# Attention kernel on one core: a unit's weighing cut into five steps of 256 columns instead of four of 128 to 512

## The reference

```python
x = x + out_proj(attention(layernorm(x)))        # 16 heads of 16, causal, 512 tokens
x = x + moe(layernorm(x))                        # 8 experts, top 2, hidden width 1024, exact GELU

scores = einsum('bhqd,bhkd->bhqk', q, k) * scale
scores = where(causal, -inf, scores)
out    = einsum('bhqk,bhkd->bhqd', softmax(scores), v)
```

## Time and profile before

| | us |
|---|---|
| timed runs, median of 3 | 976.07 |
| timed runs, lowest and highest | 970.33 and 979.5 |
| span of the profiled execution | 991.0 |
| of it PE busy | 872.7 |
| DVE busy | 722.9 |
| ACT busy | 587.6 |
| POOL busy | 461.7 |

### The profile page before, as it was taken

How to read it: one execution, slowest core, us unless ns; L and a number is a source line. 1 busy time by engine, 2 the same in 40 slices (tenths; PEclk the granted TensorE clock), 3 DMA queues, 4 the chain that set the end, 5 groups by cost and what they waited for, 6 DMA issues and landing times.

```text
span 991.0 us, 21222 instructions
## 1 busy us (share of the span) xinstructions
PE 872.7 (88%) x6870; PEld 576.0 (58%) x6870; DVE 722.9 (73%) x1658; ACT 587.6 (59%) x1079; POOL 461.7 (47%) x561
## 2 busy tenths in 40 slices
PE   4999988787788888897878898989989999999996
PEld 3655422242433434352424686879869989989875
DVE  6578878758578797969893785885766766666664
ACT  2776566656678686858776562554544455445453
POOL 2000123334425747655667546574476464544441
PEclk9999977876887978677987997999989999999998
DMA  9988667654857676575727452242223232323231
GB/s 213 293 275 256 207 180 220 177 139 120 215 168 225 172 189 183 159 191 150 201 77 232 125 120 39 46 85 51 47 36 54 50 49 46 56 50 50 36 52 19
DMA packets 146327, 130.09 MB, mean 131 GB/s; under 512 B 59344, under 2 KB 128848, under 8 KB 146096
## 3 DMA queue, kind: packets, MB, share of 16 engines
q1 hardware_dynamic: 115648, 87.51, 31.8%
q0 software_dynamic: 15680, 18.95, 12.0%
q10 hardware_dynamic: 14896, 22.28, 7.1%
HBM read 83.63 MB, written 44.80 MB: 130 GB/s over the span
## 4 chain that ended last, share of the span: by engine, by line
PE 49%; DVE 17%; issue 10%; DMA 9%; POOL 6%; SPq 5%; ACT 3%; POOLq 1%; ACTq 0%; another core or an unknown queue 0%; DVEq 0%
PE banks L769 15%; PE banks L787 14%; PE banks L582 4%; PE banks L697 3%; PE banks L685 3%; DVE arena L1230 3%; PE banks L641 2%; PE banks L572 2%; DVE weights L1384 2%; DMA weighed_values<-arena 2%; POOL out L1702 2%; DVE arena L1232 2%; POOL slot_tokens L1649 2%; PE banks L626 2%; DMA inverse_sums<-arena 2%
## 5 line engine op out<-in xcount | busy, mean ns | idle before, releaser
L991 ACT ACTIVATE arena<-banks,arena 128x256 f32<-128x256 f32 (+1 forms) x312 | 152.2, 541 | 192.9 <-issue 126.8
L769 PE MATMUL banks<-arena,weights 128*128 128x256 f16 (+1 forms) x1872 | 207.4, 266 | 11.5 <-issue 8.6
L787 PE MATMUL banks<-weights,arena 128*128 x1704 | 197.5, 275 | 3.6 <-DVE arena L1514 2.6
L769 PEld LDWEIGHTS banks<-arena,weights 128*128 x1872 | 174.0, 98 | 39.5 <-issue 16.2
L1702 POOL DMA_INDIRECT out<-arena x71 | 115.6, 1628 | 168.4 <-DVE arena L1525 131.8
L787 PEld LDWEIGHTS banks<-weights,arena 128*128 128x128 f16 x1704 | 166.4, 99 | 26.9 <-issue 6.4
L641 PE MATMUL banks<-arena 50*128 50x128 f16 (+3 forms) x512 | 126.4, 352 | 37.9 <-DMA arena<-arena 12.2
L1512 DVE TENSOR_SCALAR arena<-arena 128x512 f16<-128x512 f32 (+1 forms) x156 | 77.1, 494 | 70.6 <-ACT arena L991 58.9
L613 PE MATMUL banks<-arena 48*128 48x384 f16 (+3 forms) x512 | 103.1, 345 | 26.4 <-DVE arena L1233 9.3
L1514 DVE SCALAR_TENSOR_TENSOR arena<-arena 128x512 f16<-128x512 f32 (+1 forms) x156 | 111.0, 711 | 5.6
L641 PEld LDWEIGHTS banks<-arena 50*128 50x128 f16 x512 | 39.1, 102 | 128.7 <-issue 43.3
(11 more groups left out here) (190 smaller groups left out, 1338.9 us busy)
## 6 DMA issues: line engine op xcount, KB each, us to landing
weights<-in_L_ffn_w ACTq DMA_DIRECT2D x16, 1024.0 KB, 7.8
arena<-in_L_ffn_w SPq DMA_DIRECT2D x32, 512.0 KB
qk_parts<-weights SPq DMA_DIRECT2D x64, 128.0 KB
arena<-qk_parts SPq DMA_DIRECT2D x128, 64.0 KB, 3.2
weighed_values<-arena SPq DMA_DIRECT2D x32, 256.0 KB
token_rows<-arena SPq DMA_DIRECT2D x12, 512.0 KB, 4.3
arena<-qk_parts SPq DMA_DIRECT2D x128, 32.0 KB, 3.3
arena<-weighed_values SPq DMA_DIRECT2D x32, 128.0 KB
```

Source lines behind the costliest of these rows:

```text
L769: m = pe.matmul(bank[:, c * TILE:c * TILE + WIDTH[j]], w1[:, k, wp, f:f + P], xp[:, k, 0:WIDTH[j]], start=(i == 0), stop=(i == len(terms) ...
L787: m = pe.matmul(bank[:, c * D:(c + 1) * D], hp[:, f, c * P:(c + 1) * P], w2[:, f // (FC // 2), wp, f % (FC // 2), :], start=(f == 0 and i ...
L991: m = act.activation(h_32[r % 2][:, c, 0:WIDTH[j]], banks[:, 1 + c2, c * TILE:c * TILE + WIDTH[j]], ACT.Gelu, bias=b1_now[j % 2][:, 2 * c2 ...
```

## The change

Each unit is weighed in five steps, one behind each combined step. Step 0 and step 1 take the two halves of block 0, step 2 the first 256 columns of block 1, step 3 the last 128 columns of block 1 and the 128 of block 3, step 4 block 2. The ticks of the steps are 6, 15, 24, 33 and 43; the last unit, behind which no combined steps come, has 6, 13, 20, 27 and 34. `copy_o` goes from tick 41 to 48, `keep_o` from 51 to 55, `move_o` from 70 to 72 (not in the last unit, and `move_o` not in the last two). A step now issues eight profiled matmuls, step 3 sixteen: 48 a unit instead of 32. Waits on a number of weighings are counted in fives. The exponentials wait for just the steps that read what they overwrite.

```diff
-        W_ORDER = (0, 3, 1, 2)
+        W_STEPS = (((0, 0, 256),), ((0, 256, 512),), ((1, 0, 256),), ((1, 256, 384), (3, 0, 128)), ((2, 0, 256),))
+        W_ALL = len(W_STEPS)
+        W_READ = {0: 2, 1: 4, 3: 4, 2: 5}
...
-            for i, kt in enumerate(W_ORDER):
-                at(after + (6, 16, 24, 34)[i], "weigh", (u, kt))
-            at(after + 41, "copy_o", u)
+            last = u == UNITS - 1
+            for i in range(W_ALL):
+                at(after + ((6, 13, 20, 27, 34) if last else (6, 15, 24, 33, 43))[i], "weigh", (u, i))
+            at(after + (41 if last else 48), "copy_o", u)
...
-            at(after + 51, "keep_o", u)
-            at(after + (84 if late else 70), "move_o", u)
+            at(after + (51 if last else 55), "keep_o", u)
+            at(after + (84 if late else 72), "move_o", u)
...
-            def weigh(u, kt):
-                w.wait_ge(sem("masked"), 3 * u + (3 if kt == 2 else 2))
-                if kt == W_ORDER[0]:
+            def weigh(u, step):
+                w.wait_ge(sem("masked"), 3 * u + (3 if step == W_ALL - 1 else 2))
+                if step == 0:
...
-                for h in range(HG):
-                    a, width = PT_AT[kt], T - kt * P
-                    m = pe.matmul(banks[32 * h:32 * h + 32, O_BANK, kt * P:T], v_and_ones(u, kt, h),
-                                  p_T[u % 2][:, h, a:a + width], start=(kt == W_ORDER[0]), stop=(kt == W_ORDER[-1]),
-                                  tile_position=(0, 32 * h))
+                for kt, first_col, end_col in W_STEPS[step]:
+                    for h in range(HG):
+                        m = pe.matmul(banks[32 * h:32 * h + 32, O_BANK, kt * P + first_col:kt * P + end_col],
+                                      v_and_ones(u, kt, h), p_T[u % 2][:, h, PT_AT[kt] + first_col:PT_AT[kt] + end_col],
+                                      start=(step == 0), stop=(step == W_ALL - 1),
+                                      tile_position=(0, 32 * h), skip_group_check=True)
...
-                        w.wait_ge(sem("weighed"), TT * (u - 1))
+                        w.wait_ge(sem("weighed"), W_ALL * (u - 2) + max(W_READ[kt] for _, kt, _ in blocks))
...
-                w.wait_ge(sem("weighed"), TT * (UNITS - 1))
+                w.wait_ge(sem("weighed"), W_ALL * (UNITS - 1))
```

More of the change, by code:

```diff
@@ L886, in exponentials @@
                 for s in range(2):
+                    j, blocks = E_USES[2 * i + s]
                     if u >= 2:
-                        w.wait_ge(sem("weighed"), TT * (u - 1))
+                        w.wait_ge(sem("weighed"), W_ALL * (u - 2) + max(W_READ[kt] for _, kt, _ in blocks))
                     else:
                         w.wait_ge(sem("tops"), 2 * 2 * LATE)
-                    j, blocks = E_USES[2 * i + s]
                     w.wait_ge(sem("scored_T"), exp_use(u, 2 * i + s) + 1)
@@ L908, in copy_o @@
             def copy_o(u):
-                w.wait_ge(sem("weighed"), TT * (u + 1))
+                w.wait_ge(sem("weighed"), W_ALL * (u + 1))
                 if u > 0:
@@ L1509, in split_hidden @@
                 else:
-                    w.wait_ge(sem("weighed"), TT * UNITS)
+                    w.wait_ge(sem("weighed"), W_ALL * UNITS)
                 pair, width = slice(2 * c2, 2 * c2 + 2), slice(0, WIDTH[j])
@@ L1785, in load_v @@
                 if u >= 2:
-                    w.wait_ge(sem("weighed"), TT * (u - 1))
+                    w.wait_ge(sem("weighed"), W_ALL * (u - 1))
                 w.wait_ge(sem(f"v_store{b % 2}"), 16 * (b // 2 + 1))
```

## The result

The changed kernel takes 976.44 us (median of 20 runs, 973.28 to 984.0), the kernel before 971.9 us (20 runs, 962.09 to 979.5). The ratio is 1.0066, with a 95% interval of 1.0045 to 1.0088: 6.4 us slower, where 5.6 us faster was forecast. The time lies in the stated range, but on the other side of no change.

The account below looks back on a forecast made before the run. No engine fills attention; PE is nearest, at mean clock 0.80, DVE about as near mid-stage. +12.4 - 11 - 9 + 0 + 0 + 2 = -5.6 us on a 991.0 us span, taken as a share, gave 970.5 us; range 956 to 987.

Parts of the forecast that it names:

- The price of a step: PE's weighing in attention: 0.60 us for 256 columns at full clock, step 3 0.69 (0.60 to 0.78); +12.4 us in all.
- Part 3: PE's 17 waits at a unit's first combined step, 21.6 us, get partly filled by the added step: -11 us (0 to -17).
- Part 5: PE's wait for copy_o ahead of the next unit's first weighing stays as it is: 0, up to +6 us.
- Part 4: Fewer hollows (stretches where PE idles) in attention, so a quarter of the low-clock time goes up: -9 us (0 to -20).
- The second rival: Without the dense 512-column weighing PE's clock stays low longer in attention: +13.4 us, 989 us; chance 0.17.
- Part 7: Hand-over from attention to the experts: late loads start some 2.5 us later, partly hidden: +2 us (0 to 3).
- The first one: Rival: PE's gain in attention is waited for elsewhere, at DVE and ACT; +3.4 us, 979.4 or about 977 us; chance 0.29.
- The third one: Rival: copy_o has too short a cover before the next unit's first weighing; +0.4 us, 976.5 us; chance 0.08.
- the chance of 0.33 for faster: Chance given to the whole kernel being over 1% faster (under 966.3 us), beside same 0.46 and slower 0.21.
- the forecast's 0.46: Chance given to the main forecast of 970.5 us, own range 957 to 979, against its three rivals.

Follow-up runs that it names:

- cut_in_place: Kernel before with only the cutting: blocks 0 and 1 split, each combined step keeping its old columns behind it, 48 matmuls a unit; 1.0034 of the kernel before.
- block2_behind_fifth: Kernel before with its four uncut steps, the one of 256 columns moved from tick 34 to 40, behind the fifth combined step; 1.0028 of the kernel before.
- copy_back: Changed kernel with the fifth step at tick 40 and copy_o, keep_o and move_o at their old ticks 41, 51 and 70; 1.0049 of the kernel before.
- four_late_copy: Kernel before with its four steps, only copy_o at tick 48, keep_o at 55 and move_o at 72; 1.0015 of the kernel before.
- five_repaired: Changed kernel with copy_o, keep_o, move_o at old ticks, fifth step at 40, unit 30 at the last unit's ticks; 1.0022 of the kernel before.
- two_dense: Kernel before with its four steps at ticks 6, 6, 24, 24, so weighings stand behind the first and third combined steps only; 1.0061 of the kernel before.

## Why the prediction was wrong, step by step

- **The price of a step** was right: 0.60 us for 256 columns, and step 3 at the lower bound, 0.60. The raw cost is 9.5 us, and its reason is five separate steps a unit for four (cut_in_place), none of them the one of 512 columns that was cheap for its size. The rule of 0.21 us for each 128 columns and 0.18 on top fits three of the four forms and not 512 columns, 0.91 where it gives 1.02; the sum did not use it. The Trainium skill's rule on drains at a change of the tiling mode (TensorEngine Tiling (Array Packing), Key Properties) gave just this bound; the trace agrees that a second group in the same mode adds none (0.60 us). How much of the 0.18 us is the drain no run separates.
- **Part 3, the filled waits**, was -11 us. The waits it names did fall by 10 and 13 us, and idle ahead of first combined steps by 16 in all. The failed reasoning is "what they wait for does not depend on it". From the end of one unit's scores run at the same time the eight issues of the next load and its landing, the tops and DVE's reductions, and PE meets them at the first and at the fifth combined step. A wait filled at the first is met again at the fifth, as block2_behind_fifth shows with 25 and 10 us turned into 10 and 28.
- **Part 5, the cover of the copy**, was 0, with +6 us as its end. The wait grew from 2.6 to 10.3 us. The step that failed is the look at ACT's queue: "the copy stands at the same place against the exponentials" is true, and the stages between them, at ticks 42 to 47, were not looked up. Yet copy_back, four_late_copy and five_repaired show no cost of that wait that can be told from nothing: in copy_back ACT's work came before an exponential that PE waits for instead. Parts 3 and 5 together came to -6.8 us of idle time, against -11.
- **Part 4, the clock**, -9 us, is the step that decides the sign, and it did not come: low clock in attention 172 us in the mean of two profiles before and 176 after, and in the timed runs 0.9025 against 0.9084 and 0.9042. Without this term the forecast's own sum is +3.4 us. Nothing was measured that ties the number of hollows to the low time. That a gap ahead of a fall can be seen does not make a gain of filling it, when as much idle time turns up elsewhere. The second rival did not come either; two_dense, the opposite of the change, has 175 us.
- **Part 7, the hand-over**, was +2 (0 to 3) and measured 3 to 5: the loads start 4 us later against the end of attention and not 2.5. Behind them in SP's queue stands the write of unit 30's values, and their read-back comes 5.6 to 6.0 us behind the last weighing in the kernels with the late hand-over, 1.4 to 3.3 in both profiles of the kernel before. Which of the two delays costs the time no run separates.

With these sizes the sum is +9.5 - 6.8 + 0 + 4 = +6.7 us, beside 6.4 measured. The 4 is the middle of what the runs on the hand-over give. That the two agree to 0.3 us is luck: two profiles of one kernel differ by 4 us in idle time, and the hand-over is known to 3 at best. The runs bear out the parts by themselves: with the hand-over repaired five steps take 1.0019 and 1.0022, so all in attention together is some 2 us, neither a gain nor clearly a loss.

None of the named rivals was right as a whole. The first one's sum without the clock, +3.4, was nearest and had the right sign on the span; that the gain is waited for elsewhere is what the runs show, but the place is not DVE or ACT at their limit. The third one's sign came (10 us of waits for the copy) without its price. And the chance of 0.33 for faster does not follow from the text: somewhat under half of the forecast's 0.46 is at most 0.23.

Not tried: whether an earlier issue of the q and k loads on another queue would shorten the loop itself.

## What to carry to other kernels

Before counting a filled wait as a gain, follow the awaited thing back to where it starts: if that is an earlier point of the waiting engine's own loop, work moved within the loop only moves the wait. When a tick or a queue position is moved, list every stage of the same engine between the old and the new place, and read the one iteration that hands over to the next stage by itself; one line there was worth 3 to 5 of the 6.4 us. And before a clock share is given a price, compare the granted clock of many timed runs, or at least two profiles of the same kernel. Last, ask of an experiment whether it contains the cost it is to test: cut_in_place had the cut's matmuls and none of its PE time.

## What the runs showed of the hardware that was not expected

The granted clock's share over a stage is not a property of the kernel alone: the same program had 161.5 and 182.5 us of low clock in attention in two executions. A group of four 128x32 float32 weight sets swapped in within a step (step 3, 0.60 us for 256 columns in two groups) costs nothing on top of its columns, at the lower clock either (1.02 us for 256 columns in one group and in two), where a step of its own costs 0.18 at full clock. Two halves of 512 columns one behind the other take as long as the whole (cut_in_place, 0.91 us).
